# Softmax attention with its loops over head groups and units written out

## What is computed

```python
x = x + 0.5 * moe0(layernorm(x))            # 8 experts, top 2
x = x + softmax_attention(layernorm(x))     # 16 heads of 8 channels
x = x + 0.5 * moe0(layernorm(x))
x = x + 0.5 * moe1(layernorm(x))
x = x + decay_attention_and_gelu_ffn(layernorm(x))
x = x + 0.5 * moe1(layernorm(x))
```

```python
qkv = einsum('bsd,ed->bse', x, qkv_w) + qkv_b          # q, k, v: 16 heads, 2048 tokens, 8 channels
scores = einsum('bhqe,bhke->bhqk', q, k) / sqrt(8)
attn = softmax(scores, axis=-1)
out = einsum('bhqk,bhke->bhqe', attn, v)
out = einsum('bsd,ed->bse', out, proj_w) + proj_b
```

## Time and profile before

| | |
|---|---|
| timed runs | 1883.91, 1879.14, 1883.54 us; median 1883.54 |
| profiled execution, first to last instruction | 1880.9 us |
| its time beyond that | not on the page |
| PE busy | 1635.9 us, 87% |
| DVE busy | 1354.7 us, 72% |
| ACT busy | 836.9 us, 44% |
| POOL busy | 222.4 us, 12% |
| costliest group | L1382, DVE, the maxima: 605.2 us |
| second | L1269, PE, the first pass: 403.0 us |

### The profile page before, as it was taken

How to read it: one execution, slowest core, us unless ns; L and a number is a source line. 1 busy time by engine, 2 the same in 40 slices (tenths; PEclk the granted TensorE clock), 3 DMA queues, 4 the chain that set the end, 5 groups by cost and what they waited for, 6 DMA issues and landing times. The chain is left out here.

```text
span 1880.9 us, 23731 instructions
## 1 busy us (share of the span) xinstructions
PE 1635.9 (87%) x7285; PEld 683.8 (36%) x7285; DVE 1354.7 (72%) x1951; ACT 836.9 (44%) x1493; POOL 222.4 (12%) x145
## 2 busy tenths in 40 slices
PE   6987589999999999999998798899994356589999
PEld 3433112222222222222221443366661122256665
DVE  5776788888888778888880577666656999745654
ACT  2433427777676666667778253322223000042222
POOL 2222300000000000000000022211101324301110
PEclk8998659999999999999999899899996777799999
DMA  6000400011001100111000000000000000000000
GB/s 168 2 0 1 135 16 8 14 27 40 9 14 28 30 12 7 27 30 24 2 2 2 1 1 0 1 1 0 0 1 0 0 0 1 0 1 6 6 5 7
DMA packets 32021, 29.49 MB, mean 16 GB/s; under 512 B 7788, under 2 KB 27032, under 8 KB 31928
## 3 DMA queue, kind: packets, MB, share of 16 engines
q1 hardware_dynamic: 31928, 28.31, 5.9%
HBM read 22.13 MB, written 4.19 MB: 14 GB/s over the span
## 5 line engine op out<-in xcount | busy, mean ns | idle before, releaser
L1382 DVE TENSOR_REDUCE mx<-ps 128x1 f32<-128x1024 f32 x512 | 605.2, 1220 | 147.5 <-PE ps L1269 143.2
L1269 PE MATMUL ps<-k,q 72*128 72x512 bf16 x1024 | 403.0, 408 | 11.4 <-DVE mx L1382 9.3
L1304 PE MATMUL ps<-q,k 84*128 84x512 bf16 x1024 | 346.8, 384 | 20.7 <-ACT xn L1359 14.5
L1359 ACT ACTIVATE xT<-ps 128x512 f32<-128x512 f32 x512 | 265.1, 603 | 156.7 <-PE ps L1304 156.6
L1359 ACT ACTIVATE xn<-ps 128x512 f32<-128x512 f32 x512 | 266.2, 603 | 107.4 <-PE ps L1304 107.4
L1269 PEld LDWEIGHTS ps<-k,q 72*128 72x128 bf16 x1024 | 110.1, 115 | 331.4 <-DVE mx L1382 185.4
L854 ACT ACTIVATE silu<-ps 128x512 f32<-128x512 f32 x144 | 85.3, 596 | 265.3 <-PE ps L827 261.9
L1304 PEld LDWEIGHTS ps<-q,k 84*128 84x128 bf16 x1024 | 102.3, 102 | 185.6 <-ACT xn L1359 69.6
L889 DVE TENSOR_TENSOR hid<-ps,silu 128x512 f32<-128x512 f32 x144 | 97.8, 690 | 91.2 <-PE ps L831 89.6
L827 PE MATMUL ps<-xT,ew 128*128 (+1 forms) x288 | 151.0, 606 | 6.5 <-PEq L1750 4.8
L817 PEld LDWEIGHTS ps<-ew,hid 128*128 128x128 f32 x1152 | 138.7, 192 | 30.6 <-issue 29.9
(11 more groups left out here) (239 smaller groups left out, 1688.9 us busy)
## 6 DMA issues: line engine op xcount, KB each, us to landing
k<-k_parts SPq DMA_DIRECT2D x90, 64.0 KB
q<-q_parts SPq DMA_DIRECT2D x144, 32.0 KB
k<-k_parts SPq DMA_DIRECT2D x108, 32.0 KB
ew<-in_L_ffn_w_dram SPq DMA_DIRECT2D x2, 1024.0 KB
wraw<-in_L_ffn_w_dram SPq DMA_DIRECT2D x3, 512.0 KB, 6.7
q_parts<-part SPq DMA_DIRECT2D x4, 384.0 KB, 5.3
k_parts<-part SPq DMA_DIRECT2D x4, 384.0 KB, 2.6
v<-values SPq DMA_DIRECT2D x8, 144.0 KB, 4.2
```

Of the source, the lines that this page charges most:

```text
L1269: mm = nc.tensor.matmul(m.ps[:, S1B[i % 4], :], queries, k1[:, h, kc * CHUNK:(kc + 1) * CHUNK], start=True, stop=True)
L1304: nc.tensor.matmul(m.ps[:, S2_BANK[s], :], k2[:, h, kt * P:(kt + 1) * P], q[:, qc, h, :], start=True, stop=True).then_inc(s2_ready, 1)
L1359: nc.scalar.activation(ex[kt % P_RING][:, h, :], m.ps[:, S2_BANK[s], :], ACT.Exp).then_inc(exped, 1)
L1382: nc.vector.reduce_max(mx[:, h, qt, kc:kc + 1], m.ps[:, 2 * (i % 2):2 * (i % 2) + 2, :], AX.XY)\
```

## The change

Four loops at run time become loops of the program that writes the kernel. What was a register becomes a number, and each pass's instructions are emitted once more. On SP, PE and ACT that is four more units of code, on DVE fourteen. Operations, their order on each engine, buffers and waits stay as they are.

```diff
@@ -1213,7 +1213,7 @@
             load_maxima(0, 0)
             for qc in range(CHUNKS):
                 unit(0, qc, False)
-            with sp.Fori(1, GROUPS - 1) as g:
+            for g in range(1, GROUPS - 1):
                 for qc in range(CHUNKS):
                     unit(g, qc, False)
             for qc in range(CHUNKS):
@@ -1333,7 +1333,7 @@
             unit(0, 0, False, True)
             for qc in range(1, CHUNKS):
                 unit(0, qc, False)
-            with pe.Fori(1, GROUPS - 1) as g:
+            for g in range(1, GROUPS - 1):
                 for qc in range(CHUNKS):
                     unit(g, qc, False)
             for qc in range(CHUNKS):
@@ -1366,7 +1366,7 @@
             unit(0, 0, False, True)
             for qc in range(1, CHUNKS):
                 unit(0, qc, False)
-            with act.Fori(1, GROUPS - 1) as g:
+            for g in range(1, GROUPS - 1):
                 for qc in range(CHUNKS):
                     unit(g, qc, False)
             for qc in range(CHUNKS):
@@ -1404,7 +1404,7 @@
                 dve.wait_ge(max_turned, u + 1)
 
             maxima(0, True)
-            with dve.Fori(1, UNITS) as u:
+            for u in range(1, UNITS):
                 maxima(u)
```

## The result

The changed kernel takes 1869.97 us (median of four runs, 1868.55 to 1871.22) against 1883.72 (median of four, 1879.14 to 1884.2): ratio 0.9934, 95% interval 0.9916 to 0.9952. Timed once more beside the experiments it gave 0.9928 (0.9902 to 0.9955). The profiled execution's span is 1866.7 us with a time of 1868.55 us around it, so 1.85 us lie outside the span.

What follows compares the result with a forecast made beforehand. PE, busy 97% of the attention stage, was taken as the bound. The jump's 5.9 us and register arithmetic's 7.7, other terms 0, gave 13.6 us off the 1883.5 us median: 1870 us, range 1864 to 1877.

Steps and rivals of the forecast that it cites:

- PE's jump back: Mid attention stage: 3802 ns branch, idle and lower clock cost 5.12 us, 5.9 with two following units; goes wholly.
- ACT's jump: Same place as PE's: hidden while PE stalls, would cost 2 to 3 us if PE alone were written out.
- Register arithmetic: ACT at each key tile's head in looped units: late wait rides on register step; 0.97 us a unit, 7.7 in all.
- DVE's loop: DVE's 15 passes in attention: covered by idle time, bounds 0 and −3.5 us, taken as 0.
- The transfer queue: Key transfers in attention: nine issue in 3.0 us written out, 3.4 looped; nothing on PE waits, gain 0.
- More code to fetch: Written-out copies: up to 16 more instruction packets; 0 taken, 5.12 us for each fetch not hidden.
- The allowance: Stages behind attention: the clock may fall elsewhere when work shifts by 13.6 us; 3 us either way.
- A: Looped units: only the jump goes, the 0.97 us a unit come from something else; 1877.6 us, 8%.
- B: Jump's place: only register arithmetic goes, the 3.8 us are a fetch written-out code needs too; 1875.8 us, 5%.
- C: Written-out attention units: code fetch falls behind and starves an engine, 5.12 us a stall; slower, 1890 us with four, 4%.
- D: PE's waits for DVE in attention: all 3.5 us are gained as well; 1866.5 us, 8%.
- E: All loops: already written out before reaching the chip, so the change does nothing; 1883.5 us, 1%.

Runs made afterwards that it cites:

- only_act: Against the looped kernel before, ACT's loop alone written out; SP, PE and DVE keep theirs: 1877.24 us, ratio 0.9962.
- only_pe: Against the looped kernel before, PE's loop alone written out; SP, ACT and DVE keep theirs: 1879.84 us, ratio 0.9981.
- only_dve: Against the looped kernel before, DVE's loop alone written out: 1883.5 us, ratio 1.0003.
- only_sp: Against the looped kernel before, SP's loop alone written out: 1882.5 us, ratio 0.9992.
- swap_in_loop: Against the looped kernel before, ACT's two waits exchanged in all units, all four loops kept: 1881.94 us, ratio 0.9987.
- swap_loop_only: Against the looped kernel before, ACT's two waits exchanged in the looped units alone, all four loops kept: 1876.12 us, ratio 0.9968.
- one_pass_swap: Against the looped kernel before, two loops of one pass each on SP, PE and ACT, and ACT's two waits exchanged: 1876.61 us, ratio 0.9963.
- one_pass: Against the looped kernel before, the loop of two passes on SP, PE and ACT made two loops of one pass: 1871.18 us, ratio 0.9929.

## Why the prediction was right

The forecast was 1870 us; 1869.97 was measured, and every term of the stage can be held against a run. That they agree to 0.03 us is luck: the profiled stage gave 0.2 us less than the sum, 0.8 us came from places that had no term (the fourteenth period and the first store), and the runs scatter by more than either.

1. *PE's jump back, 5.9 us with its aftermath.* Right in mechanism: gone after the change, still there in only_act (4.99 us, and 0.45 and 1.14 in the two units behind), gone in only_pe but for ACT's part. As a number it is one draw: over their neighbours the three units cost 5.4 us in only_dve, 5.9 before and 6.1 in only_sp, where the neighbours take 48.73 us, and 6.6 in only_act, 7.4 in swap_in_loop and 8.3 in swap_loop_only, where they take 47.8. Within each three the dearer ones are those whose second unit ran longer at the lower clock: its mean granted clock is 1.00, 0.99 and 0.99, and 0.99, 0.98 and 0.95. Why quick units pay more was not tried. So the 5.9 us here and the 7.7 us of item 3 are not two prices that stand by themselves.
2. *ACT's jump, hidden, 2 to 3 us if PE alone were written out.* Right in mechanism; it costs 1.93 us there, just below.
3. *Register arithmetic, 0.97 us a unit, 7.7 in all.* Right in place and size: only_act brings 48.73 to 47.77. The reason given was half right. That the late wait rides on the register step in the loop was read rightly. That it rides on the bare wait when written out was not: there it sits on the exponential itself. So the price is not the step's 35 ns against the bare wait's 17 ns, but one more instruction between the late wait and the exponential; the exchange of the waits gives 47.80 us with all steps in place.
4. *DVE's loop, taken as 0 within 0 to −3.5 us.* Its stage is 443.05 against 443.44 us. Right.
5. *The transfer queue, 0.* Right for the stage. The 0.44 us of the fourteenth period had no term; it is mostly SP's (46.68 us with SP alone). It is smaller than the spread of the timed runs.
6. *More code to fetch, 0 and up to 16 packets more.* The time is right, the packets are not: 88 instead of 93. The runs with one loop written out say where they went. PE's alone takes q8 from 52 to 48 packets, ACT's alone takes q14 from 41 to 36, SP's changes neither, and only DVE's, whose loop has a short body, adds some (q14 45). These sum to the 88 of the changed kernel. DVE's loop with five units in its body has 54 on q14 where three units have 43. The prediction counted the copies alone and left out what a jump back over a long body fetches again. How much of the saving is that, and how much the register steps that are no longer fetched, is not separated.

The sum, 13.6 us, stands against 13.36 in the stage. The step from the sum to a time used the runs' median, and rightly: a run has 1.85 us around its span, so with as much around it the profiled execution of before would be an ordinary one, of 1882.75 us. The stages behind this one, to whose clock 3 us were given, took 844.3 and 844.2 us in these two profiles. The allowance was needed all the same: over all the profiles they take 842.1 us (one_pass_swap) to 848.5 us (swap_in_loop), with the same code there.

Of the prediction's rivals, A falls with the periods of 47.8 us, B with one_pass, C because no stall appears, D with only_dve and E with the result.

The Trainium skill's "Advanced Engine Details and Errata" ("Sequencer and Instruction Queues") would have priced the jump at 0.1 us: the runs lie somewhat below it for branches not taken (67 to 83 ns on PE) and far above it for jumps back over four units (3362 to 3942 ns in eight runs). "Runtime: NRT & Kernel Launch" ("Instruction fetch mechanics"), which has a far target fetched first, agrees with DVE's three and five units in the time (0.3 and 2.85 us) and in the instruction packets (43 and 54); no run shows from which distance on.

## What to carry to other kernels

Where one part of a stage runs looped and another written out, cut the trace into periods: the difference is the loop's price, before anything is built. In this kernel a loop at run time was dear where its body is long (the jump back) and where a late wait falls on the register step ahead of the instruction; order the waits so that the late one sits on the instruction itself, which is the opposite order in the two forms. Write out all engines whose jumps meet at one place: here PE's alone uncovered ACT's.

## What the runs showed of the hardware

- A jump back over four units of code stalls PE 3.4 to 3.9 us (eight runs) and ACT 3.1 to 3.5 us (from its branch to its next register step, eight runs); on DVE it is 0.3 us over three units and 2.85 over five, and on PE 0.21 us over the shorter pass of `moe1`.
- Gaps of similar length on PE can differ in price. A gap of 1.89 us (only_pe) cost 1.93 and the clock stayed at 2.4 GHz. One of 2.08 us (five DVE units) was followed by 2.1 us at 2.4 GHz with another gap of 0.34 us at their end, and then by matmuls at 1.2 GHz; its unit took 3.65 us longer. These are two cases, and what made the difference was not tried.
- The order of two waits in the code decides which of them the instruction carries. With the late wait on a bare wait of 17 ns, ACT stands idle 0.82 instead of 0.77 us ahead of a key tile, and a unit takes 0.51 us more.
